# Five PSUM banks dealt out anew between the maxima and the transposed scores of an attention kernel, and a small splitting step moved from VectorE to GpSimd

## The reference, cut to what matters

```
# layer 1: head size 8, q and k rotated
x = x + LN(attention1(LN(x)))
# layer 2: head size 64 (32 plain + 32 rotated), keys from a latent of 16, then 8 experts, 2 chosen
x = x + LN(attention2_and_experts(LN(x)))

scores = einsum('bhqd,bhkd->bhqk', q, k) * scale
attn   = softmax(where(causal, scores, -inf), axis=-1)   # exp(s - max over keys) / sum
out    = einsum('bhqk,bhkd->bhqd', attn, v)
```

## Time and profile before

| | |
|---|---|
| median of three runs | 577.48 us (576.83 to 578.33) |
| the profiled execution's own time | 578.05 us |
| its span | 576.0 us |
| TensorE (PE) busy | 507.3 us, 88% of the span |
| VectorE (DVE) busy | 412.2 us, 72% |
| ScalarE (ACT) busy | 313.7 us, 54% |
| GpSimd (POOL) busy | 200.6 us, 35% |
| chain of work that ended last | PE 54%, DVE 27%, ACT 10%, issue 5%, POOL 3% |

### The profile page before, as it was taken

One profiled execution on the slowest core, in us unless ns is written; L12 is line 12 of the kernel. 1 busy time (PEld: TensorE's weight loads), 2 busy tenths in 40 slices (PEclk: granted clock), 3 DMA queues, 4 the chain that ended last, 5 costly groups with the idle time before them and its releaser, 6 DMA issues.

```text
span 576.0 us, 9488 instructions
## 1 busy us (share of the span) xinstructions
PE 507.3 (88%) x3168; PEld 276.7 (48%) x3190; DVE 412.2 (72%) x1209; ACT 313.7 (54%) x586; POOL 200.6 (35%) x268
## 2 busy tenths in 40 slices
PE   7888988978899888999999999998989798899784
PEld 3433443433443344556565556554756346553643
DVE  6689898798589976876686688766476764554465
ACT  2485685767656775656756646543355342654131
POOL 5432643365236541564336414421032000410010
PEclk9999999999999999999999999999999899999978
DMA  5455524114223432448345542532203200000001
GB/s 139 128 147 172 149 82 138 43 44 135 77 80 117 155 72 90 91 115 171 103 99 108 121 127 91 129 46 52 53 15 66 55 2 1 20 2 0 2 1 37
DMA packets 29672, 47.17 MB, mean 82 GB/s; under 512 B 4648, under 2 KB 15144, under 8 KB 29112
## 3 DMA queue, kind: packets, MB, share of 16 engines
q1 hardware_dynamic: 28496, 45.72, 31.0%
q10 hardware_dynamic: 1128, 0.85, 0.7%
HBM read 27.22 MB, written 18.87 MB: 80 GB/s over the span
## 4 chain that ended last, share of the span: by engine, by line
PE 54%; DVE 27%; ACT 10%; issue 5%; POOL 3%; DVEq 0%; ACTq 0%; POOLq 0%
PE ps L612 11%; PE ps L565 9%; DVE ps L1231 8%; PE ps L686 8%; PE ps L532 6%; PE ps L530 4%; PE ps L820 3%; DVE NM L1221 3%; DVE terms L1337 2%; PE ps L550 2%; ACT PG L853 2%; PE ps L559 2%; PE ps L737 2%; PE ps L667 1%; DVE stats L1205 1%
## 5 line engine op out<-in xcount | busy, mean ns | idle before, releaser
L853 ACT ACTIVATE PG<-ps 128x512 f32<-128x512 f32 x320 | 179.4, 600 | 139.0 <-PE ps L565 87.7
L1231 DVE CUSTOM_DVE_ANT_0 ps<-ps,below 128x512 f32<-128x512 f32 (+1 forms) x256 | 157.1, 638 | 45.2 <-PE ps L532 22.6
L565 PE MATMUL ps<-QS,K 128*128 128x512 f32 x320 | 115.4, 445 | 3.0 <-ACT PG L853 2.9
L612 PE MATMUL ps<-PG,V 128*32 128x512 f32 (+3 forms) x1024 | 95.0, 444 | 3.1 <-DVE ON L1278 1.8
L532 PE MATMUL ps<-K,QS 96*128 96x256 f32 (+3 forms) x256 | 74.1, 341 | 10.2 <-DVE NM L1231 9.9
L1221 DVE TENSOR_REDUCE NM<-ps 128x2 f32<-128x512 f32 (+1 forms) x96 | 65.5, 692 | 22.1 <-PE ps L550 18.3
L530 PE MATMUL ps<-KS,QS 96*128 96x256 bf16 (+3 forms) x256 | 64.5, 303 | 17.3 <-DVE NM L1231 13.2
L565 PEld LDWEIGHTS ps<-QS,K 128*128 128x128 f32 x320 | 53.9, 189 | 44.1 <-ACT PG L853 23.1
L1066 POOL TENSOR_TENSOR rstd<-ve,half 128x4 f32<-128x4 f32 x20 | 20.4, 1018 | 117.4 <-DVE ve L1213 83.2
L1174 POOL TENSOR_SCALAR_AFFINE_SELECT PG<-PG 128x512 f32<-128x512 f32 x64 | 39.6, 641 | 57.4 <-ACT PG L853 57.0
L1167 POOL TENSOR_SCALAR_AFFINE_SELECT PG<-PG 128x512 f32<-128x512 f32 x64 | 38.7, 638 | 49.5 <-ACT PG L853 49.5
(11 more groups left out here) (170 smaller groups left out, 679.4 us busy)
## 6 DMA issues: line engine op xcount, KB each, us to landing
scr<-QC SPq DMA_DIRECT2D x24, 512.0 KB, 2.8
QS<-scr SPq DMA_DIRECT2D x64, 128.0 KB
scr<-room SPq DMA_DIRECT2D x20, 256.0 KB, 2.6
QS<-scr SPq DMA_DIRECT2D x15, 288.0 KB
KS<-scr SPq DMA_DIRECT2D x15, 288.0 KB
QS<-scr SPq DMA_DIRECT2D x64, 64.0 KB
x<-in_x SPq DMA_DIRECT2D x4, 256.0 KB, 3.3
out_x<-x SPq DMA_DIRECT2D x3, 256.0 KB, 2.3
```

The costliest lines, as they stand in the source:

```text
L565: mm = pe.matmul(bank.rearrange("p (h q) -> p h q", h=HG), keys[:, SEQ[n] % 2, P * j:P * j + P], QS2[:, heads, P * i:P * i + P], start=(ke ...
L612: mm = pe.matmul(out, v, p, start=(j == 0), stop=(j == NT - 1), skip_group_check=True)
L853: act.activation(PG[:, n % 2, unit_place(LAYER[n], (u + k) % UNITS), :], ps[:, ST0 + (u + k) % 3, :], ACT.Exp, scale=scale).then_inc(exp_d ...
L1231: dve.tensor_tensor_reduce(out=bank[:, 0:w], in0=bank[:, 0:w], in1=below[:, T - w:T], scale=-1.0, scalar=-NEG, op0=ALU.add, op1=ALU.min, a ...
```

## The change

Banks are chosen by four small functions. For the fills of layer 1 (f below 176) there are three banks, 0, 1 and 4, and fill f waits for fill f-3; for those of layer 2 two banks as before. For the units of layer 1 (u below 160) there are two banks, 2 and 3, and unit u waits for the exponential of unit u-2; layer 2's have three again, and its third unit waits until all fills of layer 1 are reduced. The split of group 0 stays on VectorE; all others move to GpSimd, in slot (n, 0), behind the first two of the four selections where the group before is of layer 1. The other two selections come behind the split.

```
+FILL_BANKS1 = (0, 1, 4)
+FILLS2, UNITS2 = FILLS * first_group(2, 0), UNITS * first_group(2, 0)
+def fill_depth(f):
+    return 3 if f < FILLS2 else 2
+def fill_bank(f):
+    return FILL_BANKS1[f % 3] if f < FILLS2 else (f - FILLS2) % 2
+def unit_depth(u):
+    return 2 if u < UNITS2 + 2 else 3
+def unit_bank(u):
+    return 2 + u % 2 if u < UNITS2 else 2 + (u - UNITS2) % 3
...
# TensorE, scores_for_max
-                if f >= 2:
-                    pe.wait_ge(fill_read, f - 1)
-                bank = ps[:, f % 2, :]
+                if f >= fill_depth(f):
+                    pe.wait_ge(fill_read, f + 1 - fill_depth(f))
+                bank = ps[:, fill_bank(f), :]
...
# TensorE, scores_for_exp
-                if u >= 3:
-                    pe.wait_ge(exp_done, u - 2)
-                bank = ps[:, ST0 + u % 3, :]
+                if u >= unit_depth(u):
+                    pe.wait_ge(exp_done, u + 1 - unit_depth(u))
+                if u == UNITS2 + 2:
+                    pe.wait_ge(fill_read, FILLS2)
+                bank = ps[:, unit_bank(u), :]
...
# GpSimd
+            def split_max(n):
+                m, done = NM[:, :, HG * (n % G):HG * (n % G) + HG], MSTEPS[n]
+                pool.wait_ge(fill_read, (n + 1) * FILLS)
+                pool.wait_ge(bank_full, BANK0["turnmax", n - 1, 0] + 1)
+                if LAYER[n] == 1:
+                    pool.tensor_copy(MB[:, :, 0, :], m).then_inc(m_step, 1)
+                    pool.wait_ge(m_step, done + 1)
+                    pool.tensor_tensor(MRest[:], m, MB[:, :, 0, :], ALU.subtract).then_inc(m_step, 1)
+                    pool.wait_ge(m_step, done + 2)
+                    pool.tensor_copy(MB[:, :, 1, :], MRest[:]).then_inc(m_step, 1)
+                    pool.wait_ge(m_step, done + 3)
+                    pool.tensor_tensor(MB[:, :, 2, :], MRest[:], MB[:, :, 1, :], ALU.subtract).then_inc(m_step, 1)
+                else:
+                    pool.tensor_copy(MF[:, :, 0, :], m).then_inc(m_step, 1)
+                    pool.wait_ge(m_step, done + 1)
+                    pool.tensor_tensor(MF[:, :, 1, :], m, MF[:, :, 0, :].bitcast(F32), ALU.subtract).then_inc(m_step, 1)
+
             def main(n, hh):
-                if hh == 0 and 1 <= n <= NG and LAYER[n - 1] == 1:
-                    causal_blocks1(n - 1)
+                masked1 = hh == 0 and 1 <= n <= NG and LAYER[n - 1] == 1
+                if masked1:
+                    causal_blocks1(n - 1, CAUSAL_ORDER[:2])
+                if hh == 0 and n >= 0 and n + 1 < NG:
+                    split_max(n + 1)
+                if masked1:
+                    causal_blocks1(n - 1, CAUSAL_ORDER[2:])
...
# VectorE, main
-                split, out = hh == 0 and 0 < n + 1 < NG, hh == 0 and 2 <= n <= NG + 1
+                out = hh == 0 and 2 <= n <= NG + 1
                 if hh == 0 and n == -1:
-                    for i in range(4):
-                        split_max(0, i)
+                    split_max0()
                 for i in range(4):
-                    if split:
-                        split_max(n + 1, i)
                     if out and i < 2:
                         divide(n - 2, i)
```

More of the change, by code:

```diff
@@ L320, in block_program @@
         ps = ctx.enter_context(nc.psum_tensor("ps", [P, 8, T], F32))
-        ST0, BK_O = 2, 5
+        BK_O = 5
         loaded_first, loaded_qkv, loaded, x_loaded = sem("loaded_first"), sem("loaded_qkv"), sem("loaded"), sem("x_loaded")
@@ L576, in scores_for_exp @@
                         pe.wait_ge(ones_ready, 1)
-                        for k in range(ST0, ST0 + 3):
+                        for k in (2, 3):
                             pe.wait_ge(bank_read[k], PRE_BANKS.count(k))
-                if u >= 3:
-                    pe.wait_ge(exp_done, u - 2)
-                bank = ps[:, ST0 + u % 3, :]
+                if u >= unit_depth(u):
[3 more added lines that the diff above has]
+                bank = ps[:, unit_bank(u), :]
                 if LAYER[n] == 2:
@@ L635, in main @@
                         pe.wait_ge(consts_ready, CONSTS)
-                        for k in range(2):
+                        for k in FILL_BANKS1:
                             pe.wait_ge(bank_read[k], PRE_BANKS.count(k))
@@ L852, in main @@
                         act.wait_ge(st_ready, u + k + 1)
-                        act.activation(PG[:, n % 2, unit_place(LAYER[n], (u + k) % UNITS), :], ps[:, ST0 + (u + k) % 3, :],
+                        act.activation(PG[:, n % 2, unit_place(LAYER[n], (u + k) % UNITS), :], ps[:, unit_bank(u + k), :],
                                        ACT.Exp, scale=scale).then_inc(exp_done, 1)
@@ L1158, in ropeB, with causal_blocks1 @@
                 pool.sem_inc(job_done[j], 1)
-            def causal_blocks1(n):
+            def causal_blocks1(n, order):
                 pair = PG[:, n % 2, 0:8, :].rearrange("p (h k) t -> p h k t", k=2)
@@ L1163, in causal_blocks1 @@
                 pool.wait_ge(exp_done, UNITS * (n + 1))
-                for j in CAUSAL_ORDER:
+                for j in order:
                     blocks = (pair[:, :, 0, 0:P], pair[:, :, 1, 0:P], both[:, :, :, 0:P], pair[:, :, 1, 3 * P:T])[j]
@@ L1226, in maximum @@
                 k = 2 * hh + hh // 2 + i
-                bank = ps[:, (n * FILLS + k) % 2, :]
+                bank = ps[:, fill_bank(n * FILLS + k), :]
                 if i < 2:
@@ L1238, in maximum, with split_max0 @@
                 reduce_fill(n, k, src, dst)
[L1240 to L1261, removed]
+            def split_max0():
+                m = NM[:, :, 0:HG]
+                dve.wait_ge(fill_read, FILLS)
+                dve.tensor_copy(MB[:, :, 0, :], m).then_inc(m_step, 1)
+                dve.wait_ge(m_step, 1)
+                dve.tensor_tensor(MRest[:], m, MB[:, :, 0, :], ALU.subtract).then_inc(m_step, 1)
+                dve.wait_ge(m_step, 2)
+                dve.tensor_copy(MB[:, :, 1, :], MRest[:]).then_inc(m_step, 1)
+                dve.wait_ge(m_step, 3)
+                dve.tensor_tensor(MB[:, :, 2, :], MRest[:], MB[:, :, 1, :], ALU.subtract).then_inc(m_step, 1)
             def divide(n, i):
```

## The result

The changed kernel takes 587.51 us (584.70 to 588.47, four runs) against 577.64 us of the kernel before beside it: ratio 1.0163, 95% interval 1.0125 to 1.0201. Put on a chip again with other kernels it gave 1.0131 (1.0066 to 1.0195). It is slower by 1.3 to 1.6%. The profiled execution took 584.70 us (span 582.4 us) at a mean granted clock of 0.969, where the one before took 578.05 us at 0.984. The other three runs of the change had 0.963, 0.960 and 0.961 and took 587.03, 588.00 and 588.47 us. The profiled execution has the most clock and is the fastest of the four: it is 6.7 us above the profiled one of the kernel before, while the medians are 9.9 us apart. The traces can account for the 6.7 only.

What follows compares the result with a forecast made beforehand. Layer 1 was taken as bound by two engines handing banks to and fro, none full, layer 2 by TensorE. 20 - 8.5 - 4 - 0.7 - 1.2 - 0.6 = +5.0 us gave 582.5 us, range 573 to 588.

Steps and rivals of the forecast that it cites:

- Part 1: At the end of layer 1's groups, unit 9 waits for unit 7's exponential, so fill 9 comes late: +20 us.
- Part 2: In layer 1, three fill banks remove fill 4's lateness in eleven groups: -8.5 us.
- Part 3: Between fill 9 and values 0 in layer 1, taking the split off VectorE shortens the way: -4 us.
- rival 1: TensorE's lateness at unit 9 is made up by the next slot 0, kernel faster: 573.1 us, chance 0.23.
- Groups 0 and 1: In groups 0 and 1, where VectorE paces the fills, moving the split gives -0.7 us.
- GpSimd's split: Four steps on GpSimd take 1.2 us (0.8 to 5.1), done before anyone needs them: 0 us.
- Rival 4: GpSimd's split is late at 1276 ns a step, 1.6 us in each of 15 groups: +24, 606 us, chance 0.03.
- Layer 2: VectorE without the split gains 1.2 us in three places; the first group takes in 0.6 us of delay.
- rival 2: Losses and gains cancel, 14.4 us lost and 14.4 won: 577.5 us, chance 0.13.
- the signs named: Layer 1: fills wait well under half of 38.8 us for VectorE, units over 35 for ScalarE, turnmax for nobody.
- Rival 3: GpSimd and VectorE block each other at a shared SBUF port, half of part 3 stays: 584.9 us, chance 0.07.

Runs made afterwards that it cites:

- e1: The kernel before with only the split moved to GpSimd, banks as before: 569.39 us against 581.91, ratio 0.978.
- e2: The kernel before with only the change's banks and waits, split still on VectorE: 590.20 us against 581.91, ratio 1.012.
- e3: The change plus idle matmuls on TensorE while it would wait for unit 7's exponential: 579.89 us against 581.91 for the kernel before, ratio 0.998.
- e10: Repeat of e1, only the split moved to GpSimd in the kernel before: 567.81 us against 581.24, ratio 0.980.
- e5: The change again, unaltered: 588.92 us against 579.10 for the kernel before, ratio 1.013.
- e6: The change with two banks instead of three for the fills, units still two: 593.95 us against 579.10 for the kernel before, ratio 1.021.
- e11: The kernel before with bank 4 lent in turns to fills and units, split left on VectorE: 572.40 us against 581.24, ratio 0.986.
- e7: The change with ScalarE's norms put behind the exponentials of units 7 to 9: 578.33 us against 579.10 for the kernel before, ratio 0.996.
- e9: Repeat of e4, bank 4 lent in turns and split on GpSimd: 567.47 us, ratio 0.979 to the kernel before.
- e4: The change with bank 4 lent in turns to fills and units, split on GpSimd: 566.45 us, ratio 0.973 to the kernel before.
- e8: e4 with ScalarE's norms put behind the exponentials too: 575.01 us against 579.10 for the kernel before, ratio 0.989.

## Why the prediction was right or wrong

The measured time lies in the range near its top (587.5 of 573 to 588), the direction was right, and the size was 5 us where 9.9 was measured. The waits came as described, the loss at unit 9 and the gain at fill 4 at the size forecast. That the kernel got slower, though, did not come out of the sum: at full clock the terms of layer 1 measure about even, and the term that tips the balance, the clock, was not in it. The direction is in this part luck. The terms, one by one:

- *Part 1, unit 9 late, +20 us.* Exit went from 37.6 to 57.9, **+20.3**. Unit 9 starts 0.65 us after the exponential of unit 7 where 0.74 was taken.
- *Part 2, fill 4, -8.5 us.* Middle went from 77.1 to 68.3, **-8.8**. The size is right and the attribution was too narrow: the split's move alone gives -7.3 (e1), the banks alone -8.7 (e2). Either suffices nearly alone: on top of the split the banks add 1.5, on top of the banks the split 0.1.
- *Part 3, the way from fill 9 to values 0, -4 us.* Here the step failed. At full clock it is **-9.3** (e3: 65.4 against 74.7). The split accounts for 2.9 of that by e1; e10, whose last entry holds a low stretch worth 1.6, gives 3.0 without it. The fills' third bank accounts for an estimated 1.4 (e5 against e6: 3.8, less two low stretches of 1.2). For the 5 us left I infer that it is the late fill 9 itself, since by then VectorE has reduced all that came before and ScalarE has caught up. In one place it can be read: between fill 9 of slot (13, 3) and the next values 0 a stage makes TensorE wait 1.24 and 1.21 us in the kernel before, and 0.93 us in e3, where that entry is 2.0 us shorter; e1 has both waits still. That is the making up of rival 1, to some quarter of the 20 us, and I had counted it as nothing.

```profile
214.94 1.10 PE L686 MATMUL ps<-xT,wabs_sb 128*128 128x512 f32 x2 [1.24 <-ACTq L884]
...
218.10 1.12 PE L686 MATMUL ps<-xT,wkva_sb 128*128 128x512 f32 x2 [1.21 <-DVEq L1430]
```

The same stage in e3, which has only the second wait:

```profile
215.82 1.12 PE L714 MATMUL ps<-xT,wkva_sb 128*128 128x512 f32 x2 [0.93 <-DVEq L1467]
```

- *The clock, not in the sum at all.* **+7.2 us** in layer 1 (e3 against the change). I priced waits at the clock of the kernel before, which never leaves its upper level in layer 1.
- *Groups 0 and 1, -0.7 us.* Fill 9 of the first group comes at 48.9 instead of 51.5 us, -2.6 in this execution; e1 and e10 have it at 51.2 and 49.7, so it varies.
- *GpSimd's split, 1.2 us, covered.* 1.06 us, covered in layer 1. Rival 4 did not happen.
- *Layer 2, -1.8 us.* From fill 9 of slot (15, 3) to the end the profiled executions took 337.3 and 337.0 us, so **-0.3**. One place took back part of the gain. Between fill 9 of slot (17, 3) and values 0 of the next group it takes 8.65 instead of 6.29 us: TensorE waits 1.80 us for the transfer that puts the maxima beside the queries, and a low stretch follows from 281 us.

```profile
280.42 1.14 PE L585 MATMUL ps<-QS,K 128*128 128x512 f32 x2 [1.80 <-DMA QS<-MP]
```

This goes with the split on GpSimd and not with the banks. The three kernels with the split on VectorE (before, e2, e11) take 6.29 to 6.30 us there, without such a wait. With it on GpSimd it is 8.65 to 9.07 us where a low stretch follows (the change, e1, e3, e5, e6, e7, e9, e10) and 7.45 and 7.52 us where none does (e4, e8). What makes the transfer late stays open.

So the sum for layer 1 at full clock would have been about even: 20.3 - 8.8 - 9.3 - 2.6 = -0.4, which is what rival 2 had; e3 indeed has the last fill 9 of layer 1's slots at 240.3 us, the kernel before at 240.8. With the 7.2 us of clock it is +6.8, and the change has that fill at 247.7. The forecast of +5 came out on the right side because a missing gain (5 us in part 3) and a missing loss (7 us of clock in layer 1's trace; 9 to 10 us by the ratios of e3 and the change) stood against each other. Of the signs named, those on the waits all came: fills 2.0 us, units 56.3, turnmax waits for nobody.

*Rival 3, the shared port.* It is seen: a 128x4 step on VectorE took 1.10 us at 126.63 and ended with the GpSimd operation beside it. The six such steps of layer 1 took 326 ns on the mean, 170 in the kernel before. It does not decide: moving the split gave 2% (e1). The Trainium skill, Perfetto Trace Analysis, section Optimizing Scalar/DVE Operations, warns that such a move might not help; in this kernel it does.

## What to carry to other kernels

Count for each bank what may stand in front of its reader, not how busy the reader is on the mean: ScalarE was the less busy engine, yet it is the one that does a 1.6 us norm between two exponentials, and the third bank bridged just that. Before a buffer is taken from one consumer for another, remove the other's own load first: with the split gone the fills needed hardly anything more. The two halves of one change were worth -2% and +1% alone and +1.3 to 1.6% together. They do not add, since both buy the same 7 to 9 us at fill 4: on top of the split's move the banks cost over 3% (0.978 and 0.980 against 1.013 and 1.016). A wait of TensorE is to be priced with the clock behind it, and where it can't be avoided, idle matmuls in it can be worth more than they cost.

## What was not expected of the hardware

The granted clock fell to its lower level for 3.4 us at waits of TensorE of 1.4 to 1.9 us, in a stretch in which it is otherwise nearly always busy. It happened five to seven times in layer 1 in each of the four profiles with two banks for the units, the norm in front and nothing in the wait (the change, e5, e2, e6), and at most once in the other nine; by e3 each cost some 1.2 us in the change. Filling the same waits with matmuls whose results are overwritten removed all of them in layer 1 of e3. The Trainium skill, Perfetto Trace Analysis, section Matmul Optimizations, says that the matmul engine scales its power by its use and that matmuls should come back to back; the traces here agree, and add the price.

A wait of that length is not enough to foretell a fall. The four profiles have 32 waits for unit 9 of 1.4 to 1.9 us, and 20 of them were followed by one or held its start. Of the 24 low stretches one came after a shorter wait for unit 9 (0.93 us, e5), two after a wait of 1.7 to 1.8 us for another stage (e2, e6), and one, in e5 from 165 us, with no idle time over 0.6 us in the ten us before it. The kernel before waits 1.77 us for a stage before 148.93, and its clock stays up. What decides it stays open.
